# A selective-scan layer: 64 unrolled steps, the convolution folded into the input projection, B applied by diagonal matrices

## What is computed

```python
xn = _layer_norm(x, ln_g, ln_b)
xz = jnp.einsum('ble,de->bld', xn, W_in)
u, z = (xz[..., :DIN], xz[..., DIN:])
up = jnp.pad(u, ((0, 0), (DCONV - 1, 0), (0, 0)))
uc = sum((conv_w[:, k] * up[:, k:k + L, :] for k in range(DCONV))) + conv_b
u = jax.nn.silu(uc)
dbc = jnp.einsum('bld,rd->blr', u, W_x)      # dt_in (8), Bm (16), Cm (16)
dt = jax.nn.softplus(jnp.einsum('blr,dr->bld', dt_in, W_dt) + dt_bias)
dA = jnp.exp(dt[..., None] * A)
dBu = dt[..., None] * Bm[:, :, None, :] * u[..., None]
# scan over l: h = dA * h + dBu; y = sum over the 16 states of h * Cm
y = y + u * D
y = y * jax.nn.silu(z)
return x + jnp.einsum('bld,ed->ble', y, W_out)
```

## Time and profile before

| | us |
|---|---|
| median of 3 runs (1648.54 to 1650.21) | 1649.15 |
| the profiled execution | 1648.05 |
| its span, first to last instruction | 1646.3 |
| mean granted TensorE clock | 0.914 of full |
| busy: TensorE, VectorE, ScalarE, GpSimd | 1350.1, 1024.8, 700.9, 398.6 |

### The profile page before, as it was taken

One profiled execution on the slowest core, in us unless ns is written; L12 is line 12 of the kernel. 1 busy time (PEld: TensorE's weight loads), 2 busy tenths in 40 slices (PEclk: granted clock), 3 DMA queues, 4 the chain that ended last, 5 costly groups with the idle time before them and its releaser, 6 DMA issues.

```text
span 1646.3 us, 24843 instructions
## 1 busy us (share of the span) xinstructions
PE 1350.1 (82%) x9010; PEld 839.1 (51%) x9062; DVE 1024.8 (62%) x2330; ACT 700.9 (43%) x1979; POOL 398.6 (24%) x313
## 2 busy tenths in 40 slices
PE   7999766887876567656897647999998999989997
PEld 4665643555554222212554434555566666656664
DVE  2556567666655688888667776755576455643334
ACT  4555324565653545453464303632234555422222
POOL 1333005444420325437400025200100333310000
PEclk9999988999998665678998969999999999999999
DMA  8000000000002200000000000000000000000000
GB/s 355 1 1 1 1 1 1 1 1 2 1 1 89 118 1 0 0 0 0 1 2 0 1 1 1 2 1 1 0 2 2 1 1 1 1 1 0 1 0 13
DMA packets 4217, 24.99 MB, mean 15 GB/s; under 512 B 1168, under 2 KB 3216, under 8 KB 3472
## 3 DMA queue, kind: packets, MB, share of 16 engines
q1 hardware_dynamic: 4112, 23.59, 3.6%
HBM read 23.06 MB, written 0.52 MB: 14 GB/s over the span
## 4 chain that ended last, share of the span: by engine, by line
PE 63%; DVE 20%; issue 8%; ACT 6%; POOL 1%; DMA 1%; DVEq 0%; SPq 0%; POOLq 0%; ACTq 0%
PE PS L1067 5%; PE PS L637 5%; PE PS L1052 4%; PE PS L1053 4%; PE PS L321 4%; PE PS L353 3%; PE PS L333 3%; PE PS L703 3%; DVE arena L2090 2%; PE PS L294 2%; PE PS L302 2%; PE PS L362 2%; PE PS L296 2%; PE PS L315 2%; PE PS L2270 1%
## 5 line engine op out<-in xcount | busy, mean ns | idle before, releaser
L545 POOL TENSOR_TENSOR arena<-arena,small 128x768 f32<-128x768 f32 (+1 forms) x64 | 107.7, 1683 | 225.7 <-DVE small L488 116.7
L873 DVE TENSOR_REDUCE arena<-PS 128x2 f32<-128x512 f32 (+1 forms) x192 | 108.8, 609 | 53.5 <-PE PS L631 52.5
L800 ACT ACTIVATE arena<-PS 128x512 f32<-128x512 f32 (+1 forms) x192 | 92.2, 532 | 107.2 <-PE PS L637 107.2
L1156 DVE TENSOR_TENSOR arena<-arena,PS 128x512 f32<-128x512 f32 x82 | 56.4, 688 | 116.0 <-ACT arena L1089 116.0
L2146 POOL TENSOR_TENSOR arena<-arena 128x512 f32<-128x512 f32 x64 | 103.9, 1643 | 89.5 <-DVE arena L2081 33.0
L1089 ACT ACTIVATE arena<-PS 128x512 f32<-128x512 f32 x82 | 49.0, 597 | 166.0 <-PE PS L1053 166.0
L425 ACT ACTIVATE arena<-PS,small 128x256 f32<-128x256 f32 (+1 forms) x256 | 110.8, 453 | 0.0
L637 PE MATMUL PS<-arena 32*128 32x256 f32 (+1 forms) x768 | 97.5, 370 | 14.0 <-DVE arena L873 8.8
L2081 DVE TENSOR_TENSOR_SCAN arena<-arena 128x512 f32<-128x512 f32 x64 | 94.0, 1473 | 21.7 <-ACT arena L1979 14.3
L1884 PE MATMUL PS<-arena,w_consts 128*128 128x512 f32 x128 | 95.1, 841 | 3.3 <-DVE arena L2090 3.3
L631 PE MATMUL PS<-arena 32*128 32x256 f32 (+1 forms) x768 | 94.5, 371 | 2.2 <-DVE arena L873 1.6
(11 more groups left out here) (408 smaller groups left out, 3121.9 us busy)
## 6 DMA issues: line engine op xcount, KB each, us to landing
w_last<-in_last SPq DMA_DIRECT2D x1, 8260.0 KB, 22.6
w_rest<-in_rest SPq DMA_DIRECT2D x1, 5898.5 KB, 36.8
w_last<-in_first SPq DMA_DIRECT2D x1, 4532.5 KB, 21.1
w_last<-in_first SPq DMA_DIRECT2D x1, 2176.0 KB, 10.1
X<-in_x SPq DMA_DIRECT2D x1, 512.0 KB, 4.5
CT<-in_ctxT SPq DMA_DIRECT2D x1, 512.0 KB, 10.8
out<-X SPq DMA_DIRECT2D x1, 512.0 KB, 3.2
w_consts<-in_consts SPq DMA_DIRECT2D x1, 373.0 KB, 3.2
```

What stands on the lines that cost most here:

```text
L545: g.tensor_tensor(p, p, ri, ALU.mult).then_inc(self.pn_done.sem, 1)
L873: v.tensor_reduce(dst, src, AX.X, ALU.max, negate=True).then_inc(self.mx_done.sem, 1)
```

## The change

The Mamba layer is written anew, with 64 unrolled steps g = 16 b + n:

- **B.** `spread_b`, the copy and GpSimd's product are replaced. dt u is transposed once per batch (`turn`, and `turned` on ScalarE), GpSimd builds diagonal matrices of B (two instructions for four steps, three groups ahead), and four fp32 matmuls per step (`drive`) put dt u B into PSUM, from where the scan reads it.
- **C** is spread in fp32 from 16 partitions; the three-part split is gone.
- **Convolution.** Its four taps are multiplied into the input weights once (GpSimd), and each half of u is four accumulated matmuls on shifted inputs; Silu reads PSUM. The skip term u D is a matmul with a diagonal matrix into the sum's bank.
- **Order.** Preparation of the next batch is spread over its predecessor's steps: inputs at n = 0, 1, 2, Silu and selections at 6 and 8, dt at 8, Abs, Relu, Exp and Ln on ScalarE at 10, the sum of the step sizes (`chain`) on VectorE at 11, transposes at 14. Gate, projection and Z of a batch are done at steps 3, 4 and 5 of the next one. Sums alternate between two PSUM banks.
- **Ends.** The layer before no longer transposes its result (`turned=False`; 20 `keep_warm` matmuls instead), the Mamba layer starts with its first two tiles, and its own `LayerEnd` is early. Weights grow by 0.6 MB.

The diff, cut to its core (`__init__`, weights' packing and removed lines left out):

```diff
     def tensor(self, pe):
-        if not self.last:
+        if self.turned:
             keep_warm(self.c, pe, self.spare, 5 if len(self.groups) == 2 else 14)
             self.transposes(pe, len(self.groups) - 1)
             keep_warm(self.c, pe, 3, 4)
+        elif not self.last:
+            keep_warm(self.c, pe, self.spare, 20)
...
+        def drive(g):
+            b, n = divmod(g, self.N)
+            if n == 0:
+                pe.wait_ge(self.tr_ev.sem, self.tr_ev.at(0, b + 1))
+            if n % 4 == 0:
+                pe.wait_ge(self.diag_ready.sem, self.diag_ready.at(0, g // 4 + 1))
...
+                pe.wait_ge(self.sc_ready.sem, self.sc_ready.at(0, g - 1))
+            for t in range(2):
+                for j in range(2):
+                    ins = pe.matmul(PS[:, 2 + g % 2, j * 256 + t * P:j * 256 + t * P + P],
+                                    self.dtuT[:, b % 2, t, j * P:(j + 1) * P], self.diag[:, g % 12 * 2 + t, :],
+                                    start=True, stop=True, skip_group_check=True)
+            ins.then_inc(self.db_done.sem, 1)
+
+        def spread(g):
...
+            if g >= 2:
+                pe.wait_ge(self.hc_ready.sem, self.hc_ready.at(0, g - 1))
+            pe.matmul(PS[:, 4 + g % 2, 0:256], self.onehot[32:48, n:n + 1].to_broadcast([16, P]),
+                      self.CB[32:48, b % 2, :], start=True, stop=True).then_inc(self.c_done.sem, 1)
...
+        transposes(0, 2, 2, 4)
         inputs(0, 0)
+        inputs(0, 1)
+        inputs(0, 2)
+        transposes(2, 4, 3, 0)
+        transposes(6, 2, 4, 2)
+        selections(0)
+        keep_warm(c, pe, 5, 2)
+        steps(0)
+        keep_warm(c, pe, 5, 36)
+        turn(0)
+        drive(0)
+        spread(0)
+        for i in range(self.G):
+            b, n = divmod(i, self.N)
+            if i + 1 < self.G:
+                drive(i + 1)
+                spread(i + 1)
+            if i >= 2:
+                add(i - 2)
+            if b and n == 4:
+                outputs(b - 1)
+            if b + 1 < B:
+                if n < 3:
+                    inputs(b + 1, n)
+                if n == 6:
+                    selections(b + 1)
+                if n == 8:
+                    steps(b + 1)
+                if n == 14:
+                    turn(b + 1)
...
+        def logs(b):
+            a.wait_ge(self.dt_done.sem, self.dt_done.at(0, b + 1))
+            for j in range(2):
...
+                ins = a.activation(self.ab[:, s], PS[:, 1, s], ACT.Abs, bias=self.bdt[:, j:j + 1], scale=1.0)
...
+                ins = a.activation(self.rl[:, s], PS[:, 1, s], ACT.Relu, bias=self.bdt[:, j:j + 1], scale=1.0)
...
+            a.activation(self.ex, self.ab, ACT.Exp, scale=-1.0).then_inc(self.ex_ready.sem, 1)
...
+            a.activation(self.lw, self.ex, ACT.Ln, bias=c.one, scale=1.0).then_inc(self.lw_ready.sem, 1)
...
+            if g >= 4:
+                a.wait_ge(self.sc_ready.sem, self.sc_ready.at(0, g - 3))
...
+            if n == 1 and b:
+                turned(b)
+            if b + 1 < B:
+                if n == 6:
+                    silus(b + 1)
+                if n == 8:
+                    selections(b + 1)
+                if n == 10:
+                    logs(b + 1)
+            elif n == 10:
+                self.end.root(a, 0)
...
+    def chain(self, eng, b):
...
+        eng.tensor_scalar(self.r, self.ex, 1.0, 1.0, ALU.add, ALU.subtract).then_inc(self.chain_step.sem, 1)
...
+        eng.tensor_tensor(self.r, self.ex, self.r, ALU.subtract).then_inc(self.chain_step.sem, 1)
...
+        eng.tensor_tensor(self.r, self.r, self.rl, ALU.add).then_inc(self.chain_step.sem, 1)
...
+        eng.tensor_tensor(self.dt[:, b % 2, :], self.r, self.lw, ALU.add).then_inc(self.chain_step.sem, 1)
...
+        eng.tensor_tensor(self.dtu, self.dt[:, b % 2, :], self.u[:, b % 2, :], ALU.mult)\
+            .then_inc(self.chain_step.sem, 1)
...
+        for g in range(self.G):
+            b, n = divmod(g, self.N)
+            scan(g)
+            if g:
+                outputs(g - 1)
+            if b and n == 3:
+                gate(b - 1)
+            if b and n == 5:
+                finish(b - 1)
+            if b + 1 < B and n == 11:
+                self.chain(v, b + 1)
+            if b == B - 1 and n == 8:
+                self.end.early_stats(v)
+            if b == B - 1 and n == 13:
+                self.end.tiles(v, 0)
```

More of the change, by code:

```diff
@@ L121, in __init__ @@
         self.x_ready = self.sig("x_ready", 2, 1)
+        self.x_tile = None
         self.arena_free = None
@@ L143, with __init__ @@
 class LayerEnd:
-    def __init__(self, c, z_ready, last=False, early=False, counted=0, reload=False, spare=3):
-        self.spare = spare
+    def __init__(self, c, z_ready, last=False, early=False, counted=0, reload=False, spare=3, turned=True):
+        self.spare, self.turned = spare, turned and not last
         self.c, self.z_ready, self.last, self.reload = c, z_ready, last, reload
@@ L200, in transposes @@
         c = self.c
-        for n in range(*self.groups[g]) if not self.last else ():
+        for n in range(*self.groups[g]) if self.turned else ():
             pe.wait_ge(self.x_tile.sem, self.x_tile.at(0, n + 1))
@@ L214, in vector @@
         self.tiles(v, g)
-        if not self.last and g == 0:
+        if self.turned and g == 0:
             v.wait_ge(self.xt_ps.sem, self.xt_ps.at(0, 1))
@@ L220, in scalar @@
         c, g = self.c, len(self.groups) - 1
-        if g == 1 and not self.last:
+        if g == 1 and self.turned:
             a.wait_ge(self.xt_ps.sem, self.xt_ps.at(0, 1))
@@ new lines, in add @@
+        def add(g):
+            b, n = divmod(g, self.N)
+            bank = 6 + b % 2
+            if n == 0 and b >= 2:
+                pe.wait_ge(self.z_ready.sem, self.z_ready.at(b - 2, 1))
+            pe.wait_ge(self.hc_ready.sem, self.hc_ready.at(0, g + 1))
+            pe.matmul(PS[:, bank, :], c.ident, self.hC[:, g % 3, :], start=(n == 0), stop=(n == self.N - 1),
+                      skip_group_check=True).then_inc(self.acc_done.sem, 1)
+            if n == 0:
+                for j in range(2):
+                    pe.matmul(PS[:, bank, j * 256:j * 256 + 256], self.Ddiag[:, j, :],
+                              self.u[:, b % 2, j * 256:j * 256 + 256], start=False, stop=False, skip_group_check=True)
@@ L1997, in scalar @@
[L1997 to L2005 removed]
+        for k, (i, j) in enumerate(((0, 2), (2, T))):
+            a.wait_ge(self.var_ready.sem, self.var_ready.at(0, k + 1))
+            c.act.link(a, a.activation(c.ln[:, i:j], c.mv[:, i:j, 1], ACT.Ln, bias=c.eps, scale=1.0))
+            a.activation(c.rs[:, i:j], c.ln[:, i:j], ACT.Exp, scale=-0.5).then_inc(self.rs_ready.sem, 1)
@@ new lines, in scalar @@
+        normal(0, 2, 0, 1)
+        silus(0)
+        normal(1, 3, 1, 2)
+        normal(2, 4, 3, 1)
+        selections(0)
+        logs(0)
+        for g in range(self.G):
+            b, n = divmod(g, self.N)
+            if g == 0:
+                decays(0)
+                turned(0)
+            else:
+                decays(g)
+            if n == 1 and b:
[9 more added lines that the diff above has]
+                self.end.root(a, 0)
@@ L2119, in vector @@
-        for j in range(2):
-            for k in range(4):
-                convolve(0, 0, j, k)
-        arguments(0, 0)
-        parts(0, 0)
-        steps_of_time(0, 0)
-        with v.Fori(0, B - 1) as it:
-            c.dve.enter(it)
-            batch(it, True)
-        c.dve.leave(B - 1)
-        batch(B - 1, False)
+        for i, j in ((0, 2), (2, T)):
+            if self.x_tile is not None:
+                v.wait_ge(self.x_tile.sem, self.x_tile.at(0, j))
+            for n in range(i, j):
+                ins = v.bn_stats(c.bn[:, n, :], c.X[:, n, :])
+            link(ins)
+            for n in range(i, j):
+                ins = v.bn_aggr(c.mv[:, n, :], c.bn[:, n, :])
+            ins.then_inc(self.var_ready.sem, 1)
@@ new lines, in finish @@
+        def finish(b):
+            v.wait_ge(self.o_done.sem, self.o_done.at(0, b + 1))
+            v.scalar_tensor_tensor(c.Z[:, 2 * b:2 * b + 2, :], c.X[:, 2 * b:2 * b + 2, :], 2.0,
+                                   two(PS[:, 6 + b % 2, 0:256]), ALU.mult, ALU.add).then_inc(self.z_ready.sem, 1)
+        for g in range(self.G):
+            b, n = divmod(g, self.N)
+            scan(g)
[11 more added lines that the diff above has]
+                self.end.tiles(v, 0)
@@ L2130, in vector @@
+        outputs(self.G - 1)
+        gate(B - 1)
+        finish(B - 1)
         v.wait_ge(self.z_ready.sem, self.z_ready.at(B - 1, 1))
```

517 lines of the change are left out of this document (213 added, 304 removed).

## The result

The changed kernel is **slower**, by 0.24%: 1652.63 us (median of 9 runs, 1650.65 to 1653.97) against 1648.54 (9 runs, 1647.02 to 1650.21). The ratio is 1.0024, its 95% interval 1.0013 to 1.0034. The prediction said 1639 us and gave slower a chance of 0.27. The profiled execution took 1653.29 us (span 1651.5) where the prediction's sum came to 1638.15.

The account below looks back on a forecast made before the run. VectorE bounds the layer now, TensorE after the change. Front -5.7, three batches -5.6, last batch +7.1 and tail -5.7 give -9.9 us: 1638 us profiled, 1639 against the median; range 1620 to 1662, the forecast's own 1630 to 1646.

Parts of the forecast that it names:

- the upper end of 1.44: VectorE's scan reading one operand from PSUM: 1.23 us taken, 1.44 us beside GpSimd's diagonals as the upper end.
- the hidden diagonals: GpSimd builds diagonals for four steps in 4.3 us out of 9.2 us, three groups ahead, so nothing waits for them.
- the wait at step 11: Per batch, VectorE waits 3.5 us for ScalarE's decays before the scan of step 11, behind the next batch's logarithm.
- the chain behind it: VectorE's sum of step sizes at step 11: 3.3 us, less 0.4 slack, 2.9 us per batch; 5.2 us to the next scan.
- no drain behind a table load: ScalarE's table loads cost 1.28 us each without an added drain; the rival, as much again, 1647 us, had chance 0.03.
- the start of the layer: From the layer before's end at 528.1 to the first scan at 555.5 instead of 561.15: 5.7 us saved.
- The plain step: One scan step, bound by TensorE: records of 0.90 + 0.43 + 0.85 = 2.18 us, taken as 2.3 us.
- issue and empty queues: Rival: every TensorE group starts with an empty queue, steps of 2.51 us, +13 us, 1652 us; chance 0.12.
- The waits are mostly satisfied early: The prediction's argument against steps of 2.51 us: TensorE's groups would seldom start with an empty queue.
- a little over one such step per batch, 2.5 us: Loss to TensorE's lower clock near two standstills of about 3 us; half clock adds 2.18 us to a step.
- The rival that made it 14 steps: Lower clock after each pair of standstills, 14 of 64 steps: +30.5 - 7.5, 1662 us; chance 0.20.
- The tail: From the last scan to the next layer's input: 5.4 + 3.6 = 9.0 us instead of 14.68, 5.7 us saved.

## Why the prediction was wrong

**Right, in place and size:** the scan (1.22, and 1.22 beside GpSimd, so the upper end of 1.44 did not come); the hidden diagonals; the wait at step 11 (3.43 against 3.5) and the chain behind it (5.16 against 5.2); no drain behind a table load (Ln starts at 589.54, 0.02 us after its load ends); the weights in time, though they took 38.6 us; the engine that bounds.

**Right by luck:** the start of the layer (555.65 against 555.5; its own terms add up to 555.7). The 3 us allowed for the lower clock were not lost to it there: the clock from 528 us on was 0.94, not 0.65. Instead the last statistics of the layer before came at 527.22 and not at 525.57, 1.65 us of it, and the input products began at 535.27 and not at 533.2.

**The plain step failed.** "So I take 2.3 us per step" rested on records from stretches in which all matmuls have 128 rows, and was laid against a new product of 16. The step measured 2.57, beyond the upper end of 2.51 that the prediction had set. The rival "issue and empty queues" had the right time (1652 us) by luck: it added 13 us for the step and nothing for clock and tail, while the batches without loss of clock missed by 5.4 in all. It also had the wrong cause: its price was that of groups whose weight loads are in the open, 1.01 + 0.54 + 0.96 us, and that is what happened (0.99 + 0.62 + 0.96), but not for the waits, which cost nothing, as the run with more of them showed. "The waits are mostly satisfied early" was true and was no argument against it. The 16-row shape stood in the diff. Sixteen steps at 0.27 us above the forecast are 4.3 us a batch; the second and third missed by 2.5 without loss of clock (56.6 against 54.1), so other terms of them were some 1.8 us too large. These are the two waits: 3.5 + 2.9 us were charged, but at full clock the two distances were 2.66 and 2.60 us over a plain step, and the scan behind them came 0.65 earlier than in one, 4.6 us together. The wait of 3.43 us holds 0.77 of idle time that VectorE has in every plain step. The first came out 1.0 under 54.1: it has no predecessor to finish, and its first three steps take 1.71, 3.42 and 3.44 us instead of 2.57, 4.30 and 4.29.

**The clock was mis-sized.** The mechanism was put in its place, two standstills close together at steps 11 and 12, and "a little over one such step per batch, 2.5 us" was too few. It cost 3.2, 4.7 and 4.7 us, between five and six steps in all, at 4.86 instead of 2.57 us each, where three were counted. The rival that made it 14 steps, over 30 us, was too many. Each standstill was priced by its own length, and the clock apart from them; taking away one gave back most of the clock as well, which is why the table load is worth 7.2 us per batch and not 2.5. What brings the clock down is not settled by the runs. In two of three batches of the changed kernel it fell behind the first standstill of 2.04 us, before the second; the same one alone (chain in five pieces) was followed by a fall in one of three, the other one alone (one table set, 2.14 us) in none of three, and a single longer one with the chain in the tenth step (3.26 and 4.01 us) by one in every batch. With 128 rows it fell behind the first one of 2.78 us in two batches, and behind the second of 2.71 us in the third. So neither the pair nor the length of one decides it alone.

**The tail** was taken from the end of the layer before (the earlier trace rows and two tiles at 0.60 us), where nothing ran on GpSimd. There GpSimd stands idle for 30.19 us, until its first diagonals at 543.84. Here its clearing meets the tiles of X, and this is 2.1 of the 3.65 us missed. The kernel before has it too, in small: the first of its eight tiles took 1.06 us, the median one 0.34, and it was done 0.1 us after the clearing (781.36). There the statistics of eight tiles had let most of the clearing pass; with two tiles only, X came earlier into it. Another 1.4 us are TensorE's sums: they run two steps behind the scans, so that four of them, 3.70 us from 776.40 on, stand between the last spread and the gate at 780.14, where the prediction put the gate one sum behind the last product (775.85 + 1.9 + 1.0 = 778.75).

Summed, the three steps that failed are 4.1 + 1.3 us (step), 5.1 (clock) and 3.65 (tail); with 0.15 and 0.8 they are the 15.1.

## What to carry to other kernels

Where TensorE bounds a loop, give every matmul in it the same number of rows, if need be by zero rows. Products of 16 and of 8 rows between ones of 128 each made their step 0.4 us longer here, and the added rows cost nothing. Put serial work of another engine between the steps in pieces no longer than that engine's idle time per step, and not as a block. Look for TensorE's pauses: behind those of 1.5 to 2.5 us here the lower clock cost up to 4.7 us a batch, where each of the waits cost 2.6. And when an engine's last work moves, look at what the next layer's engines do at that time.

## What the runs showed of the hardware

- A product of 16 rows between products of 128 made a step of six fp32 products 0.39 us longer, 0.10 in going in, 0.19 in the product and 0.10 behind it (0.99, 0.62, 0.96 against 0.89, 0.43, 0.86 us). With a product of 8 rows the step was 0.38 us longer (3.46 against 3.08 us).
- A satisfied wait ahead of a matmul group took no time that the trace shows (2.57 us with and without).
- Behind TensorE pauses of 2.04 us and 1.49 to 2.52 us, 5.2 us from spread to spread, steps took 4.86 us at a clock of 0.50, and in two of three batches the clock was down already between the two. With spare matmuls in them it stayed at 1.00, with the second alone (2.14 us) too; with the first alone (2.04 us) the batches had 1.00, 0.97 and 1.00. Single pauses of 3.26 and 4.01 us were followed by the lower clock in each of three batches, one of 2.78 in two of three.
- A VectorE sum with both inputs in SBUF took 1.34 us instead of 0.69 beside a GpSimd product, a scan with one input in PSUM 1.22 in either case, and the scalings of two tiles 2.64 and 2.44 us instead of 0.34 beside a GpSimd clearing of 3.51 us.
